# Masks among the product tiles, one head's maxima among the sums, adds in two transfers: a graph layer with experts on one core

## The reference, cut to what matters

```python
h = (x @ W).reshape(n, H, C)                       # layer 1: 4 heads of 192, layer 2: 2 heads of 96
e = leaky_relu(s_src[src] + s_dst[dst], 0.2)
emax = segment_max(e, dst, num_segments=n)
ee = exp(e - emax[dst]); denom = segment_sum(ee, dst)
out = segment_sum(ee / denom[dst] * h[src], dst) + bias
...
combined = concat([x, out2]) @ Wu + bu
...
h = silu(einsum('th,eih->tei', flat, w1)); outs = einsum('tei,ehi->teh', h, w2)
combined = (sel * balanced[..., None]).sum(axis=1)  # the two chosen experts of each token
```

## Time and profile before

| | |
|---|---|
| median of 3 runs | 1066.67 us (1063.98 to 1069.22) |
| the profiled execution's own time | 1061.51 us |
| its span | 1059.8 us |
| PE busy | 925.7 us, 87% |
| DVE busy | 627.1 us, 59% |
| ACT busy | 386.2 us, 36% |
| POOL busy | 389.6 us, 37% |

### The profile page before, as it was taken

One profiled execution on the slowest core, in us unless ns is written; L12 is line 12 of the kernel. 1 busy time (PEld: TensorE's weight loads), 2 busy tenths in 40 slices (PEclk: granted clock), 3 DMA queues, 4 the chain that ended last, 5 costly groups with the idle time before them and its releaser, 6 DMA issues.

```text
span 1059.8 us, 13855 instructions
## 1 busy us (share of the span) xinstructions
PE 925.7 (87%) x5064; PEld 785.8 (74%) x5064; DVE 627.1 (59%) x1222; ACT 386.2 (36%) x575; POOL 389.6 (37%) x302
## 2 busy tenths in 40 slices
PE   3899899999999999999189999897888469999993
PEld 3798785786678899999088988886877457666672
DVE  7676995602078132386989999695996763222221
ACT  2543330223344000244576766346863401121120
POOL 3058888888888874000110000000000313434441
PEclk9999999969999999999589999989988759999997
DMA  9994579333226449600140000216005924666664
GB/s 315 232 161 83 96 203 263 51 45 45 1 1 145 63 92 287 200 2 1 51 149 23 1 1 1 88 63 208 2 1 199 363 60 91 119 120 119 120 120 60
DMA packets 78417, 112.43 MB, mean 106 GB/s; under 512 B 34994, under 2 KB 53933, under 8 KB 78351
## 3 DMA queue, kind: packets, MB, share of 16 engines
q0 software_dynamic: 35264, 39.86, 22.9%
q1 hardware_dynamic: 40781, 65.39, 19.2%
q10 hardware_dynamic: 2306, 6.29, 1.5%
HBM read 80.02 MB, written 31.49 MB: 105 GB/s over the span
## 4 chain that ended last, share of the span: by engine, by line
PE 53%; DVE 20%; DMA 16%; issue 6%; ACT 2%; SPq 1%; POOL 0%; POOLq 0%; DVEq 0%; ACTq 0%
PE bank L1621 41%; DMA out<-orow,send 14%; PE bank L1890 9%; DVE pbuf L1399 4%; DVE pbuf L1373 3%; DVE sb_before L1318 3%; DVE junk_k L1194 2%; PE bank L1632 2%; DVE h L1382 2%; DMA keyrow<-key_d 2%; SPq L552 1%; DVE o L1382 1%; PE bank L1826 0%; DVE sb_stats L1142 0%; DVE xnT_lo L1118 0%
## 5 line engine op out<-in xcount | busy, mean ns | idle before, releaser
L661 POOL DMA_INDIRECT table<-match_n,slot_ix x168 | 276.2, 1644 | 90.2 <-issue 48.9
L1890 PE MATMUL bank<-h,pbuf 128*128 128x197 f32 (+1 forms) x1200 | 194.5, 324 | 29.6 <-DVE pbuf L1399 28.6
L1890 PEld LDWEIGHTS bank<-h,pbuf 128*128 128x128 f32 x1200 | 186.7, 199 | 37.4 <-DVE pbuf L1399 34.2
L1194 DVE SCALAR_TENSOR_TENSOR junk_k<-keyrow,key,sb_before 128x384 uint8<-128x384 f32 x168 | 92.7, 614 | 21.8 <-DMA keyrow<-key_d 11.5
L1318 DVE CUSTOM_DVE_ANT_0 sb_before<-a_row,pen 128x1280 bf16<-128x1280 f32 x60 | 89.4, 1491 | 27.3 <-ACT pen L958 11.2
L1606 DVE TENSOR_SCALAR orow<-bank,gates 128x384 f32<-128x384 f32 x54 | 33.4, 618 | 115.8 <-PE bank L1621 115.8
L692 POOL IOTA cst_i<- 128x128 int32 x1 | 0.2, 229 | 271.8 <-DVE o L1382 271.8
L1016 ACT ACTIVATE pbuf<-pbuf 128x1280 f32<-128x1280 f32 x60 | 76.1, 1269 | 64.4 <-DVE pbuf L1373 64.4
L1399 DVE SCALAR_TENSOR_TENSOR pbuf<-pbuf,cnt 128x1280 f32<-128x1280 f32 x60 | 88.7, 1485 | 0.0
L1621 PE MATMUL bank<-xnT_hi,w_hi 128*128 128x512 f32 (+1 forms) x216 | 85.1, 394 | 3.7 <-DVE xnT_lo L1118 2.8
L728 POOL DMA_INDIRECT out<-orow,send x27 | 42.9, 1587 | 111.5 <-DMA out<-orow,send 92.5
(11 more groups left out here) (346 smaller groups left out, 1668.4 us busy)
## 6 DMA issues: line engine op xcount, KB each, us to landing
keyrow<-key_d SPq DMA_DIRECT2D x28, 384.0 KB
cnt<-table POOLq DMA_DIRECT2D x20, 320.0 KB, 9.3
f_all<-in_w1T SPq DMA_DIRECT2D x8, 768.0 KB, 10.6
f_all<-in_w2T SPq DMA_DIRECT2D x8, 768.0 KB, 12.2
u_row<-m_d POOLq DMA_DIRECT2D x8, 640.0 KB, 6.3
w_raw<-in_kqvT SPq DMA_DIRECT2D x4, 1152.0 KB
acc_d<-ubuf SPq DMA_DIRECT2D x20, 192.0 KB, 2.6
x<-acc_d SPq DMA_DIRECT2D x10, 384.0 KB, 6.1
```

Source lines behind the costliest of these rows:

```text
L661: pool.indirect_dma_start(table[i], bass.IndirectOffsetOnAxis(ap=slot_ix[:, g:g + 1], axis=0), match_n[:, g:g + 1], None, compute_op=ALU.a ...
L1194: nc.vector.scalar_tensor_tensor(out=junk_k[g % 2][:, :], in0=keyrow[c % KR][:, w:w + KW * P], scalar=key[:, g:g + 1], in1=before[:, first ...
L1890: ins = nc.tensor.matmul(b[:, d * stride:d * stride + v.shape[-1]], score[:, dt * P:(dt + 1) * P], v, start=st == 0 and d == 0, stop=st == ...
```

## The change

- Masks: three are made earlier, and the last six in pairs after tiles (1, 0) to (1, 2) (`PEN_AT` is a table now). The bias row and ACT's split of the last weight half come one tile earlier.
- The low part of that half is made by POOL in two instructions (multiply by the gain, subtract) instead of six of DVE. POOL also takes over the subtraction `wuo_lo` between the layers.
- Maxima: dt 4 to 9 for heads 0 and 1 together, then head 2, and head 3's six between units 2, 5, 8, 11, 14 and 17 of the sums, its shifts after unit 18. Head 3's shift row is written from `ucol` by SP directly.
- The turned shift rows of heads 0, 1 and 2 come after tiles (1, 5), (1, 6) and (1, 8); DVE copies heads 0 and 1 out together, head 2 after unit 0. POOL waits for head 2's last maximum before it loads head 0's row.
- ACT's -128 steps lie between tiles (1, 3) to (1, 9) (`LESS_AT`); DVE's bias steps (L1409 to L1416) come after unit 1.
- Between the layers "wuT" and "rsum" come ahead of "aR" on PE and ACT; ACT starts to leak after head 0's maxima, and copies head 1's rows after units 2 and 3.
- Experts: an add becomes two of half rows, each with its own count of landings; `send` holds two lists of places.
- Some unused semaphores go, `MAX1` follows the new count of maxima, `bias_of_layer` and `spread_row` only move.

```diff
@@ -349,8 +349,9 @@
                 reserve(*name)
-        PEN_AT = [(0, 2), (0, 4), (0, 7), (0, 8), (1, 0), (1, 1), (1, 2), (1, 3), (1, 4), (1, 5)]
-        ROWS_AT = {(1, 6): 0, (1, 9): 1}
+        PEN_AT = {(0, 2): [0], (0, 3): [1], (0, 4): [2], (0, 6): [3], (1, 0): [4, 5], (1, 1): [6, 7], (1, 2): [8, 9]}
+        ROWS_AT = {(1, 5): 0, (1, 6): 1, (1, 8): 2}
+        LESS_AT = {(1, 3): [0], (1, 4): [1, 2], (1, 5): [3], (1, 6): [4, 5], (1, 7): [6], (1, 8): [7, 8], (1, 9): [9]}
         for hf in range(2):
...
@@ -591,6 +591,9 @@
             sp.dma_start(wuo_raw[:, :, 0:D], Wu[D:, :].rearrange("(k p) n -> p k n", p=C2)).then_inc(g_in, 16)
+            sp.wait_ge(m_done, H1)
+            sp.dma_start(m_d[2 * (H1 - 1) * NT:2 * H1 * NT, :].rearrange("(k t) p -> p k t", k=2), ucol[:, H1 - 1, :, :],
+                         allow_slow_non_contiguous=True).then_inc(m_out[H1 - 1], 16)
             finished(sp, "agg", H1 - 1, 4)
...
@@ -609,7 +612,8 @@
             sp.wait_ge(out_sent, 16 * NT)
-            sp.wait_ge(added_out, 16 * NP_)
+            for i in range(2):
+                sp.wait_ge(added_out[i], 16 * NP_)
...
@@ -676,18 +680,32 @@
+            pool.wait_ge(w_hi_done, SPLITS.index(A0 + 1) + 1)
+            finished(pool, "wb", 1)
+            i, gain = SLOT[A0 + 1], gb_c[:, 0, :].unsqueeze(2).broadcast_to([P, KD, HALF])
+            nc.gpsimd.tensor_tensor(w_raw[i][:, :, :], w_raw[i][:, :, :], gain, ALU.mult).then_inc(gain_done, 1)
+            pool.wait_ge(gain_done, 1)
+            ins = nc.gpsimd.tensor_tensor(w_lo[i][:, :, :], w_raw[i][:, :, :], w_hi[i][:, :, :].bitcast(F32), ALU.subtract)
+            ins.then_inc(w_split, 1)
             for h in range(H1):
-                evacuated(pool, "mT", h)
-                pool.dma_start(m_d[2 * h * NT:2 * (h + 1) * NT, :], mrow[h % 2][:, :]).then_inc(m_out[h], 16)
                 if h == 2:
+                    pool.wait_ge(max_done, NT + NT - 4)
                     pool.dma_start(u1_row[0][:, :], row_of(m_d, 0)).then_inc(u_row_in[0], 16)
                     pool.dma_start(u2_row[0][:, :], row_of(m_d, 1)).then_inc(u_row_in[0], 16)
-                pool.wait_ge(m_out[h], 16)
+                if h < H1 - 1:
+                    evacuated(pool, "mT", h)
+                    pool.dma_start(m_d[2 * h * NT:2 * (h + 1) * NT, :], mrow[h % 2][:, :]).then_inc(m_out[h], 16)
+                if h < H1 - 1:
+                    pool.wait_ge(m_out[h], 16)
             finished(pool, "h1", 1, NT - 1)
             for h in range(1, H1):
+                if h == H1 - 1:
+                    pool.wait_ge(m_out[h], 16)
                 pool.dma_start(u1_row[h][:, :], row_of(m_d, 2 * h)).then_inc(u_row_in[h], 16)
...
+            pool.wait_ge(g_hi_done, 1)
+            nc.gpsimd.tensor_tensor(wuo_lo[:, :, :], wuo_raw[:, :, :], wuo_hi[:, :, :].bitcast(F32), ALU.subtract).then_inc(g_split, 1)
             evacuated_all(pool, "agg2")
...
@@ -718,21 +736,24 @@
-            def send_rows(a):
+            half_rows = out.rearrange("n (h c) -> (n h) c", h=2)
+
+            def send_rows(a, hf):
                 if a == 0:
...
                 else:
-                    pool.wait_ge(added_out, 16 * a)
-                pool.wait_ge(orow_done, 2 * (a + 1))
-                pool.indirect_dma_start(out, bass.IndirectOffsetOnAxis(ap=send[:, a:a + 1], axis=0), orow[a % 3][:, :], None,
-                                        compute_op=ALU.add, bounds_check=N - 1).then_inc(added_out, 16)
+                    pool.wait_ge(added_out[hf], 16 * a)
+                pool.wait_ge(orow_done, 2 * a + hf + 1)
+                pool.indirect_dma_start(half_rows, bass.IndirectOffsetOnAxis(ap=send[:, hf, a:a + 1], axis=0),
+                                        orow[a % 3][:, hf * HALF:(hf + 1) * HALF], None,
+                                        compute_op=ALU.add, bounds_check=2 * N - 1).then_inc(added_out[hf], 16)
...
                 if a >= 3:
-                    send_rows(a - 3)
+                    send_rows(a - 3, 0), send_rows(a - 3, 1)
...
@@ -972,20 +993,19 @@
                     h1_out(hf, t)
-                    if (hf, t) in PEN_AT:
-                        dt = PEN_AT.index((hf, t))
+                    for dt in PEN_AT.get((hf, t), ()):
                         if dt == 4:
...
                         mask(dt, 0), mask(dt, 1)
+                    if (hf, t) == (0, 4):
+                        split_gain_hi(act, A0 + 1)
                     if (hf, t) == (0, 5):
-                        split_gain_hi(act, A0 + 1)
-                    if (hf, t) == (0, 6):
                         weight_rows(1)
-            for i in range(NT):
-                nc.scalar.activation(cnt[i][:, :], cnt[i][:, :], ACT.Identity, bias=less_c[:, 0:1]).then_inc(cnt_done, 1)
+                    for i in LESS_AT.get((hf, t), ()):
+                        nc.scalar.activation(cnt[i][:, :], cnt[i][:, :], ACT.Identity, bias=less_c[:, 0:1]).then_inc(cnt_done, 1)
...
@@ -1014,12 +1034,11 @@
                     nc.scalar.activation(pbuf[i % 3][:, :], pbuf[i % 3][:, :], ACT.Exp).then_inc(e_done, 1)
-
-            attention(0, H1, u2_row, row_ready_1)
-
-
-            for h in range(H2):
-                rows_out("aR", (), h, a2_row[h])
+                    between(i)
+
+            attention(0, H1, u2_row, row_ready_1, lambda i: None)
+
+
             act.wait_ge(g_in, 16)
...
@@ -1027,11 +1046,13 @@
                                          ACT.Copy).then_inc(free("wuT", k, m), 1)
+            nc.scalar.activation(lr[:, NT, :], finished(act, "rsum")[:, 0:EM], ACT.Copy).then_inc(free("rsum"), 1)
+            for h in range(H2):
+                rows_out("aR", (), h, a2_row[h])
             b = finished(act, "wuR")
...
             nc.scalar.activation(wuo_hi[:, :, :], wuo_raw[:, :, :], ACT.Copy).then_inc(g_hi_done, 1)
-            nc.scalar.activation(lr[:, NT, :], finished(act, "rsum")[:, 0:EM], ACT.Copy).then_inc(free("rsum"), 1)
             for t in range(NT + 1):
...
@@ -1048,10 +1069,13 @@
                                  ACT.Copy).then_inc(free("lr"), 1)
-            rows_out("uR2", (0,), 1, u1_row_b[1])
-            rows_out("uR2", (1,), 1, u2_row_b[1])
-            act.wait_ge(max_done, MAX1 + 2 * NT)
-            attention(H1, H2, u2_row_b, row_ready_2)
+            act.wait_ge(max_done, MAX1 + NT)
+
+            def rows_between(i):
+                if i in (2, 3):
+                    rows_out("uR2", (i - 2,), 1, (u1_row_b, u2_row_b)[i - 2][1])
+
+            attention(H1, H2, u2_row_b, row_ready_2, rows_between)
...
@@ -1315,6 +1339,8 @@
                 for h in hs:
+                    if rows_a is a_row and dt == 0:
+                        dve.wait_ge(a_in[h], 16)
                     ins = nc.vector.tensor_tensor_reduce(
...
@@ -1332,25 +1358,40 @@
                 evacuated(dve, "pen", dt, 0), evacuated(dve, "pen", dt, 1)
-                if dt == 0:
-                    for h in range(H1):
-                        dve.wait_ge(a_in[h], 16)
                 masked_max(pen[dt], a_row, range(H1), dt)
-                if dt == 1:
-                    split_gain_lo(dve, A0 + 1)
-            for h in range(H1):
-                for dt in range(4, NT):
-                    if h == 0:
-                        evacuated(dve, "pen", dt, 0), evacuated(dve, "pen", dt, 1)
-                    masked_max(pen[dt], a_row, (h,), dt)
-                dve.wait_ge(max_done, 4 + (h + 1) * (NT - 4))
-                leaky_max(H1, h, 1)
+            def max_row_out(h):
                 b = finished(dve, "mT", h)
...
-            def attention(h0, heads, row_ready, u1_r, stride, chans, out_rows, added, stage, nbank, per):
+            for dt in range(4, NT):
+                evacuated(dve, "pen", dt, 0), evacuated(dve, "pen", dt, 1)
+                masked_max(pen[dt], a_row, (0, 1), dt)
+            dve.wait_ge(max_done, NT)
+            leaky_max(H1, 0, 1), leaky_max(H1, 1, 1)
+            for dt in range(4, NT):
+                if dt == 7:
+                    max_row_out(0), max_row_out(1)
+                masked_max(pen[dt], a_row, (2,), dt)
+            dve.wait_ge(max_done, NT + NT - 4)
+            leaky_max(H1, 2, 1)
+
+            def between_first(i):
+                if i == 0:
+                    max_row_out(2)
+                if i == 1:
+                    bias_of_layer()
+                if i % 3 == 2 and i < 18:
+                    masked_max(pen[4 + i // 3], a_row, (3,), 4 + i // 3)
+                if i == 18:
+                    dve.wait_ge(max_done, MAX1)
+                    leaky_max(H1, 3, 1)
+
+            def between_second(i):
+                pass
+
+            def attention(h0, heads, row_ready, u1_r, stride, chans, out_rows, added, stage, nbank, per, between):
...
@@ -1592,16 +1635,17 @@
                     step(nc.vector.tensor_tensor(list_f[:, :], list_f[:, :], db[:, NP_:2 * NP_], ALU.add))
-                    nc.vector.tensor_copy(send[:, :], list_f[:, :]).then_inc(send_done, 1)
```

(36 more changed lines are left out.)

68 lines of the change are left out of this document (35 added, 33 removed).

## The result

The kernel after takes 1039.5 us in the median of 4 runs (1038.1 to 1040.9), the kernel before 1067.1 in the same comparison: ratio 0.974, 95% interval 0.9715 to 0.977. It is 2.6% faster; the forecast was 1041.5. The profiled execution of after has a span of 1036.3 and a time of 1038.1.

What follows compares the result with a forecast made beforehand. PE's products were taken as most of the chain, with three places where PE doesn't set the pace. 12.0 - 5.0 + 7.7 + 10.2 = 25 us gave 1036.5 profiled, 1041.5 on the median's scale; range 1027 to 1056.

Steps and rivals of the forecast that it cites:

- A: From the product tiles to the first layer's first score: that score comes 12.0 us earlier, ends 9 and 18.
- the blocking: Before the first score: DVE stands still during POOL's two instructions of 5.9 us each, 11.8 us in all.
- The second path: Before the first score: PE's waits for head shifts, then ACT's last steps, end at 517.9, as late as the main path.
- 5.0 given back: First layer's sums: head 3's maxima moved between score steps, with small steps, cost 5.0 us; ends 2 and 12.
- B: Between the layers: second layer's first score 9.2 us earlier, less 1.5 for copies, net 7.7; ends 4 and 12.
- the subtraction on POOL: Between the layers: POOL's wuo_lo, at most 4.0 us after DVE's last shift set, ends at 724.4, just in time.
- the term of 1.5 lost by the copies between units: Second layer's sums: six ACT row copies between units 2 and 3 cost DVE 1.5 us.
- C: Expert adds at the end: half-row adds cut the pitch from 6.5 to 6.2 us, gaining 10.2; ends 3 and 14.
- (2): Rival on the experts: split adds bring only their tail, the fetch holds pitch at 6.5; 15 us gained, 1052; chance 0.17.
- (3): Rival: POOL and DVE don't exclude each other in long instructions, PE stays at full clock; 37 us gained, 1029; chance 0.15.
- (4): Rival on the experts: half adds land in 7.2 us or more, pitch 8, kernel slower at 1096; chance 0.04.
- (5): Rival: maxima among the sums fully exposed, POOL's split holds PE at (1, 0), adds gain nothing; 1060; chance 0.04.

Runs made afterwards that it cites:

- e3: Kernel after with five of head 3's six maxima taken before the first score and the sixth after unit 2: 1034.7 us, ratio 0.972 to before.
- e9: Kernel after, run again unchanged: 1040.5 us.
- e1: Kernel after with each add of expert rows whole again, one transfer instead of two halves: 1049.7 us, ratio 0.985 to before.
- e10: Kernel before, run again unchanged: 1071.3 us.
- e11: Kernel before, run once more unchanged: 1071.1 us.
- e5: Kernel before with only the adds of expert rows split into halves: 1057.1 us against 1069.7, ratio 0.989.
- e2: Kernel after with the low part of the last weight half made on DVE again instead of POOL: 1036.6 us, ratio 0.972 to before.
- e12: Kernel after with the last weight half's low part on DVE, five of head 3's maxima before the first score, wuo_lo on POOL after all maxima: 1029.0 us, ratio 0.9626.

## Why the prediction was right, step by step

- **A, 12.0 earlier; 14.5 measured** (94.7 to 80.2). The order of events was right: POOL's two instructions at 461 to 472, tile (1, 0), DVE's last work, then the fetch of head 0's row. The term that was too large is the blocking: 11.8 forecast, 3.71 + 4.85 = 8.6 measured, since POOL's two took 11.1 together and DVE worked 2.5 of them, at the edges and while POOL itself stood. Here the Trainium skill's rule ("SBUF — State Buffer", Who interferes with whom: the shared port pair is an exclusive lock) held for instructions of this length, in both directions. The same skill's figure ("GPSIMD Engine Reference", section 3.1) scales by an estimate to 5.06 for 2304 and 3.42 for 1556 elements; without the wait for DVE's running maximum the rows give 472.29 - 467.26 = 5.03 and, alone, 3.46. My 5.9 was too high. The rest was as worked out: the fetch took 6.2 for 5.95. The end of 1.3 lost at (1, 0) did not come. The second path was as long as forecast, 0.21 short of the first. What the prediction didn't ask is whether head 3's maxima could stay beside the fetch: five of them cost 0.6 there (e3).
- **5.0 given back; 5.9 measured.** By the times of DVE's scores, before and after: the maxima behind units 2, 5 and 8 cost 2.3 together, that behind unit 17 0.9 (forecast 3.1 for these four), unit 11 1.4 (1.5), unit 14 0.9 (0.3: I took it for nearly hidden, and it isn't), the first three units with their small steps 0.3 (0.1). That head 3's row could be written in 2560 pieces without harm was right: issued at 596.83, POOL went on behind it at 613.36, 16.2 after the issue had ended (596.83 + 0.37), and DVE's first score of head 3 came at 633.5.
- **B, 9.2 to the first score less 1.5; 7.2 and, behind it, 3.3 gained measured** (42.7 for 49.9, and 143.3 for 146.6; 145.0 in e9). The step that failed is the subtraction on POOL. I priced it at the end of DVE's maxima; it ran as soon as ACT was done, beside the fifth maximum, and cost 3.15 there, then 1.6 of clock. The relay's start came 4.9 earlier instead of 4.1, and the first score 7.2 instead of 9.2. In exchange the term of 1.5 lost by the copies between units came out as 0.9 gained up to unit 16. The copies do cost: DVE's scores of units 4 and 5 come 1.0 later against those before them, 0.70 of it a wait for ACT. But moving them away from the front let PE start sooner: it stood 6.32 before its first unit in before and then took 7.03 for 40 products; in after it stands 1.59 and takes 2.47 for 20, and the score of unit 3 comes 1.9 earlier. The sum had no term for this. Most of the remaining 2.4 is the clock at units 16 to 18, and luck of the profile of after.
- **C, 10.2; 8.8 between the two first profiles, 8.3 between e1 and after, 12 against e10 and e11; some 11 by the ratios of e1 and e5.** POOL's rhythm and the waits are those of the sum; the fetch lands in 4.6, the better of the two cases I left open, and the pitch is 6.11 for 6.2.
- **Rivals.** (2), a fetch that holds the pitch at 6.5, falls by PE's 1.0 us of waits for it. (3) falls by e2 and e12: the engines do exclude each other. (4) needs half adds that land in 7 or more: they land in 4.4 (e5) and 4.3 (e9). (5) falls by e1 and e5, by tile (1, 0), which isn't late, and by the 5.9, where six fully exposed maxima were put at 12.
- **The scale, and luck.** The profiled execution of before was 5.2 us short of its median, for which I carried 0.5%, and 9.7 short of e10 and e11, mostly in two stretches (5.7 up to the first tile, 3.6 in the experts). Without the first tile the stages of after and e9 give 14.3 - 5.9 + 7.2 + 2.6 + 12.0 = 30 against e10 and e11, and those of after 27.9 against the first profile; the medians of the two comparisons that hold both kernels say 27.6 and 29.1. That the two first spans differ by 23.5, close to the 25 forecast, is in part luck: the terms were off by +2.5 (A), -0.9 (given back), -2.0 and +4.8 (B), -1.4 (C), and the first tile took 4.4. The mechanisms of A and C held; in B one step failed and two gains weren't in the sum.
